# Opening of the linear attention: another order of norm, projections and evictions, with an early activation

## The chip, the core and the metric

The kernel runs on one core of a Trainium2 chip. The metric is the device time of one execution in microseconds (us). The engines of the core work beside each other and meet only at semaphores: PE (TensorE, matmuls and transposes; PEld is its weight load), DVE (VectorE), ACT (ScalarE), POOL (GpSimd) and SP (SyncE, which issues the DMAs). Each executes its own instructions strictly in the order of the program.

## The reference, cut to what matters

```python
def attn_a(hidden_states, ...):                        # hidden_states: layernorm(x), (2, 1024, 256)
    qkv = jax.nn.silu(hidden_states @ qkv_w.T)         # 32 heads of q, k and v, 64 each
    ...                                                # linear attention over blocks, with decays
    attn = _rmsnorm(attn, norm_w)
    gate = jax.nn.sigmoid(hidden_states @ gate_w.T)
    return gate * attn @ out_w.T

x = L0_attn_a_hidden_states                            # (2, 1024, 256) float32
x = x + attn_a(_layernorm(x), ...)                     # the stage of this change
x = x + ffn(_layernorm(x), ...)
x = x + attn_b(_layernorm(x), ...)
x = x + ffn(_layernorm(x), ...)
```

`_layernorm` subtracts the mean over the 256 features and divides by sqrt(variance + 1e-5).

## The kernel before

The 2048 tokens lie in SBUF as X, 16 tiles of 128 tokens by 256 features, in four blocks of four tiles (512 tokens). Every product of float32 matrices is made of three matmuls: each operand is split into a high part (rounded to the format that TensorE takes at full rate) and a low part (what the rounding left), and high by high, high by low and low by high are summed.

**The norm** (`norm_steps`) has a step for each block b and engine. `sync` loads the block. `moments` (DVE) takes statistics of four tiles (L84) and aggregates them (L87). `deviation` (ACT) takes the square root of the four variances (L93). `normalise` (DVE) takes the reciprocal (L97) and writes (x - mean) / deviation for four tiles (L100); in this stage the result lies in the buffer of the queries, so that the trace calls it la_q. `turn` (PE) transposes the four tiles in two halves of the features (L113), 8 transposes, into PSUM banks that are named la_Y and la_O in turn. `high` (ACT) copies both banks to a_hTh (L121), `low` (DVE) subtracts it from the bank and writes a_hTl (L127).

**The linear attention** (`linear_attention`) goes through 8 quads of heads, each in four steps of 512 tokens. A step needs projections (`project` on PE, L539) of kinds k, q, v and g (keys, queries, values, gate), in halves n = 0 and 1: k, q and g take 6 wide matmuls a half, v takes 12 of half the width. They alternate between two PSUM banks la_R. ACT evicts a bank (`evict`: L310 for k, L312 for q, L305 for v, L308 for g), through Silu or Tanh; the next use of that bank waits for it on the semaphore `silu_ok`. The weights of a quad come in four pieces (`PIECES`: queries and keys, values, gate, output). Each is split by `split` on ACT (L373, high part, semaphore `wh_ok`) and `low` on POOL (L245, low part, `wl_ok`). The projection of k waits for the first piece, that of v for the second.

ACT holds the functions of its activations in tables. The square root lies in another set than Silu and Tanh, so that an `ACT_TABLE_LOAD` stands in the program wherever it changes from the one to the other; plain copies need none.

**The order** is written out by hand for each engine: an opening in a straight line (the ends of the blocks `scalar`, `vector`, `tensor`, `gpsimd` before their loops), then a loop of units, one for each step. In the opening DVE norms block 0 and block 1 and then takes the low parts of block 0; PE turns both blocks, projects k and q of step 0 (four halves), turns block 2, computes scores, and projects v of step 0. ACT evicts these four halves after the deviation of block 3 and the split of the second piece. POOL takes the low part of the second piece only when all four blocks are normed (`h_ok`, NT = 16), and after it the decayed queries. SP issues in this order: block 0, the identity, the first piece of weights, block 1, the other pieces, the decays C, block 2, block 3.

Of the kernel before, what the change touches and what calls it, by code (L numbers as in the profile page):

```python
# [4 lines left out]
F32 = mybir.dt.float32  # L5
# [4 lines left out]
ACT = mybir.ActivationFunctionType  # L10
AXX = mybir.AxisListType.X

P = 128
BATCH, SEQ, HID = 2, 1024, 256
TOK = BATCH * SEQ
NT = TOK // P
KT = HID // P
TB = 512
NTB = TOK // TB
# [29 lines left out]
def norm_steps(nc, ctx, mem, name, X, ident, hTh, hTl, banks, load=None, norm=True, H=None):  # L49
# [4 lines left out]
    sb = lambda n, s, d: mem.enter_context(nc.sbuf_tensor(name + n, s, d))  # L54
    sem = lambda n: ctx.enter_context(nc.semaphore(name + n))
    if norm:
        stats = sb("stats", [P, NT, 6], F32)
        mv = sb("mv", [P, NT, 2], F32)
        std = sb("std", [P, NT], F32)
        rstd = sb("rstd", [P, NT], F32)  # L60
        epst = sb("epst", [P, 1], F32)
        eps_ok, stats_ok, mv_ok, std_ok = sem("eps_ok"), sem("stats_ok"), sem("mv_ok"), sem("std_ok")
        rstd_ok, h_ok = sem("rstd_ok"), sem("h_ok")
# [14 lines left out]
    def moments(dve, b):  # L78
# [6 lines left out]
        for t in range(TPB * b, TPB * (b + 1)):  # L85
            dve.wait_ge(stats_ok, t + 1)
            dve.bn_aggr(mv[:, t, :], stats[:, t, :]).then_inc(mv_ok, 1)  # L87

# [44 lines left out]
    return {"sync": sync, "moments": moments, "deviation": deviation, "normalise": normalise, "turn": turn,  # L133
# [3 lines left out]
def linear_attention(nc, ctx, X, ident, ident_in, hTh, hTl, hidden, w_quads, c_quads, ln2, fin, WF, w_ffn, q_ffn):  # L137

    with ExitStack() as mem:
        sb = lambda n, s, d: mem.enter_context(nc.sbuf_tensor("la_" + n, s, d))  # L140
# [100 lines left out]
        def _(pool):  # L241
# [36 lines left out]

            low(0, 0, 1)
# [20 lines left out]
        def _(act):  # L300
# [74 lines left out]
            for b in range(2):  # L375
                ln["deviation"](act, b)
            act.wait_ge(w0_in[0], 16)
            split(0)
            ln["high"](act, 0)
            ln["deviation"](act, 2)  # L380
            ln["high"](act, 1)
            ln["deviation"](act, 3)
            act.wait_ge(w0_in[1], 16)
            split(1)
            for n in range(4):
                evict(0, 0, "kq"[n // 2], n % 2, n)
# [30 lines left out]
        def _(dve):  # L417
# [91 lines left out]
            ln["moments"](dve, 0)  # L509
            ln["moments"](dve, 1)  # L510
            ln["normalise"](dve, 0)
            ln["normalise"](dve, 1)
            ln["low"](dve, 0)
            ln["moments"](dve, 2)
            ln["low"](dve, 1)
            ln["moments"](dve, 3)
            ln["normalise"](dve, 2)
            ln["normalise"](dve, 3)
            ln["low"](dve, 2)
# [15 lines left out]
        def _(pe):  # L535
# [168 lines left out]
            ln["turn"](pe, 0)  # L704
            ln["turn"](pe, 1)
            ln["ready"](pe, 0)
            for n in range(4):
                if n >= 2:
                    pe.wait_ge(silu_ok, n - 1)
                project(0, 0, "kq"[n // 2], n % 2)  # L710
# [1093 lines left out]
```

## Time and profile before

| | us |
|---|---|
| median of 3 runs | 1226.91 (1225.04 to 1227.93) |
| the profiled execution, its own time | 1230.14 |
| its span | 1228.1 |
| PE busy | 1123.5 (91%) |
| DVE busy | 652.6 (53%) |
| ACT busy | 594.7 (48%) |
| POOL busy | 486.8 (40%) |

The span is what the profiler saw from the first to the last instruction of that one execution. Busy times overlap, and a busy PE is not a PE at its peak, since matmuls are pipelined. PE carries most of the kernel; the exceptions are places where it waits for another engine, and the opening is one: in the first of forty equal slices of the span, PE is busy for four tenths, in the others mostly for nine or more.

### The profile page before, as it was taken

To read this page: it belongs to the slowest core of one execution; us is meant where nothing else is said; L and a number is where in the kernel's file an instruction comes from. 1 tells how busy PE (TensorE), PEld (TensorE's weight loads), DVE (VectorE), ACT (ScalarE), POOL (GpSimd) and SP (SyncE) were. 2 spreads that over 40 slices of the span, in tenths; PEclk is the share of its full clock that TensorE was granted. 3 is DMA by queue.
4 is the path that set the end of the run, shared out by engine and by line. 5 is a ranking of instruction groups with operands and counts; after the bars stand their busy time and mean duration, and the time that the engine had idled before them with its cause. 6 is when DMAs were issued, how large, how long until landed. Compare 5 with 4: busy or idle time off the path is not lost. (4 is left out here: it accounts for less than half of the span.)

```text
span 1228.1 us, 33277 instructions
## 1 busy us (share of the span) xinstructions
PE 1123.5 (91%) x14272; PEld 869.4 (71%) x14272; DVE 652.6 (53%) x1397; ACT 594.7 (48%) x1112; POOL 486.8 (40%) x513
## 2 busy tenths in 40 slices
PE   4999999999999999999987895894799999998698
PEld 3888888888888888888876785771344444436587
DVE  5243342433425455454467537885777777743742
ACT  3544444444445455554453442331367666774442
POOL 1445453454535546455453363104122222221255
PEclk8999999999999999999997897895899999999899
DMA  3100001001010020210301002155122222000001
GB/s 120 52 2 22 32 3 45 9 20 39 3 45 28 16 77 16 71 35 15 118 11 39 1 1 86 52 154 130 29 53 53 53 54 53 2 2 1 1 18 52
DMA packets 15805, 49.57 MB, mean 40 GB/s; under 512 B 2416, under 2 KB 7088, under 8 KB 12976
## 3 DMA queue, kind: packets, MB, share of 16 engines
q1 hardware_dynamic: 15664, 47.50, 13.3%
q8 instruction: 112, 1.84, 0.6%
q14 instruction: 29, 0.24, 0.1%
HBM read 36.54 MB, written 10.75 MB: 39 GB/s over the span
## 5 line engine op out<-in xcount | busy, mean ns | idle before, releaser
L1591 DVE TENSOR_REDUCE ca_mx<-ca_S 128x1 f32<-128x640 f32 (+1 forms) x192 | 177.4, 955 | 53.9 <-PE ca_S L1461 51.1
L1556 ACT ACTIVATE ca_PT<-ca_ST 128x512 f32<-128x512 f32 (+1 forms) x304 | 159.1, 578 | 81.2 <-PE ca_ST L1485 78.2
L451 DVE SCALAR_TENSOR_TENSOR la_y<-la_g,la_O 128x512 f32<-128x512 f32 x64 | 41.1, 684 | 221.6 <-PE la_O L627 221.6
L539 PE MATMUL la_R<-a_hTh,WF 128*128 128x512 f32 x384 | 131.0, 406 | 3.0 <-ACT la_k L310 3.0
L1432 POOL TENSOR_SCALAR_AFFINE_SELECT ca_PT<-ca_PT 128x256 f32<-128x256 f32 (+1 forms) x112 | 48.8, 442 | 193.0 <-ACT ca_PT L1556 192.7
L265 POOL TENSOR_TENSOR la_yl<-la_y,la_yh 128x512 fp32r<-128x512 f32 x64 | 81.8, 1299 | 94.5 <-ACT la_yh L339 94.5
L253 POOL TENSOR_TENSOR la_qd<-la_q,la_C 128x512 f32<-128x512 f32 x64 | 80.9, 1284 | 85.3 <-PE la_O L627 80.5
L458 DVE TENSOR_TENSOR X<-la_R,X 128x512 f32<-128x512 f32 x64 | 44.2, 691 | 119.8 <-PE la_R L539 119.7
L936 POOL TENSOR_TENSOR f_fl<-f_f,f_fh 128x512 fp32r<-128x512 f32 x48 | 62.5, 1308 | 112.2 <-ACT f_fh L840 112.2
L305 ACT ACTIVATE la_v<-la_R 128x512 f32<-128x512 f32 x64 | 38.3, 598 | 112.8 <-PE la_R L539 112.8
L442 DVE SCALAR_TENSOR_TENSOR la_S<-la_S,la_C,la_Y 128x64 f32<-128x64 f32 x448 | 88.7, 275 | 0.2
L539 PEld LDWEIGHTS la_R<-a_hTh,WF 128*128 128x128 f32 x384 | 74.1, 193 | 20.4 <-ACT la_k L310 3.5
L271 POOL TENSOR_TENSOR fin_sqacc<-fin_sqacc,la_sq 128x512 f32<-128x512 f32 x64 | 86.3, 1348 | 4.6
L312 ACT ACTIVATE la_q<-la_R 128x512 f32<-128x512 f32 x64 | 38.3, 599 | 102.7 <-PE la_R L539 102.7
L1499 PE MATMUL ca_OB<-ca_PT,V 128*32 128x512 f32 (+3 forms) x768 | 82.7, 502 | 3.2 <-POOL ca_PT L1432 1.6
L539 PE MATMUL la_R<-a_hTh,la_Wh 128*128 128x512 f32 x192 | 77.7, 405 | 0.0
L539 PE MATMUL la_R<-a_hTl,WF 128*128 128x512 f32 x192 | 76.8, 400 | 0.0
L539 PE MATMUL la_R<-a_hTh,la_Wl 128*128 128x512 f32 x192 | 76.2, 397 | 0.0
L539 PE MATMUL la_R<-a_hTl,la_Wh 128*128 128x512 f32 x192 | 75.9, 395 | 0.0
L1485 PE MATMUL ca_ST<-ca_QS,ca_KS 99*128 99x512 bf16 (+3 forms) x240 | 61.7, 328 | 3.2 <-ACT ca_PT L1556 1.4
L901 DVE SCALAR_TENSOR_TENSOR f_f<-f_U,SCL,f_sg 128x512 f32<-128x512 f32 x48 | 35.6, 748 | 51.8 <-PE f_U L789 40.2
L1458 PE MATMUL ca_S<-ca_KS,ca_QS 96*128 96x512 bf16 (+2 forms) x240 | 61.3, 329 | 2.0 <-DVE ca_mx L1591 1.9
(214 smaller groups left out, 2909.5 us busy)
## 6 DMA issues: line engine op xcount, KB each, us to landing
la_Wraw<-w_quads_dram SPq DMA_DIRECT2D x7, 1280.0 KB, 6.6
q_parts<-rp_QP SPq DMA_DIRECT2D x4, 768.0 KB, 3.7
k_parts<-rp_KP SPq DMA_DIRECT2D x4, 768.0 KB, 3.5
ca_KS<-k_parts SPq DMA_DIRECT2D x10, 256.0 KB, 6.8
qw_w<-w_ffn_dram SPq DMA_DIRECT2D x12, 192.0 KB, 2.4
q_ffn<-qw_w SPq DMA_DIRECT2D x12, 192.0 KB, 1.9
X<-hidden_dram SPq DMA_DIRECT2D x4, 512.0 KB, 7.3
out_dram<-X SPq DMA_DIRECT2D x8, 256.0 KB, 2.0
```

The costliest lines, as they stand in the source:

```text
L253: pool.tensor_tensor(qd[:, pr, :].rearrange("p (c t) -> p c t", t=CH), q[:, j % 4, pr, :].rearrange("p (c t) -> p c t", t=CH), C[:, slot, ...
L265: pool.tensor_tensor(yl[:, pr, :], y[:, pr, :], yh[:, pr, :].bitcast(F32), ALU.subtract).then_inc(yl_ok, 1)
L271: pool.tensor_tensor(sqacc[:, tok], sqacc[:, tok], sq[:, pr, :], ALU.add).then_inc(sqa_ok, 1)
L442: ins = dve.scalar_tensor_tensor(S[:, at, pr, :], S[:, at - 1, pr, :], C[:, slot, C_B + pr:C_B + pr + 1], U, ALU.mult, ALU.add)
L539: m = pe.matmul(out, a, b, start=n == 0, stop=n == len(pairs) - 1)
L936: pool.tensor_tensor(fl[:, tb % 2, it, :], f[:, n % 2, :], fh[:, tb % 2, it, :].bitcast(F32), ALU.subtract).then_inc(fl_ok, 1)
L1432: pool.affine_select(part, part, [[0, max(nh, 2)], [1, P]], ALU.is_ge, 0.0, base=0, channel_multiplier=-1).then_inc(cut_ok, 1)
L1458: ins = pe.matmul(bank[:, col:col + k1 - k0], Q[0:SROWS, j, qt * P:(qt + 1) * P], K[0:SROWS, j, k0:k1], start=True, stop=True)
L1485: ins = pe.matmul(ST[at % NB][:, e * w:(e + 1) * w], KS[g % NSL][0:KROWS, h + e, kt * P:(kt + 1) * P], QS[g % NSL][0:KROWS, h + e, q0:q0 + ...
L1499: ins = pe.matmul(OB[32 * j:32 * j + 32, q0 - qb * TB:q0 - qb * TB + w], V[:, 8 * (g % 2) + kt, HG * (g // 2) + j, :], PT[:, (NM2 * g + b) ...
L1556: act.activation(PT[:, (NM2 * g + b) % NPT, h:h + nh, 0:w], ST[at % NB][:, 0:nh * w].rearrange("p (h q) -> p h q", h=nh), ACT.Exp, scale=S ...
L1591: dve.reduce_max(out, src, AXX).then_inc(s1_free, 1)
```

## The change

Only the opening of the linear attention is touched; the loops and the other stages are the same.

- A new tile `root` (one number per partition) and a new step `table` of the norm: one activation with the square root of `epst`, which nobody reads. ACT begins with it.
- ACT: split of the first piece, then the deviation of block 1, the high parts of block 0, the deviations of blocks 2 and 3; then the evictions of k, the high parts of block 1, the evictions of q, and only then the split of the second piece.
- DVE: block 0 is normed before the moments of block 1; the moments of block 2 come before the low parts of block 0; then the moments of block 3 and the norms of blocks 1, 2 and 3; the low parts of block 1 follow them.
- PE: turns block 0 and projects k, then turns block 1 and projects q.
- POOL: its first split waits until block 0 is normed (`h_ok`, NT // NTB = 4).

```diff
@@ norm_steps
+    def table(act):
+        act.wait_ge(eps_ok, 1)
+        act.activation(root[:], epst[:], ACT.Sqrt, bias=epst[:])
@@ gpsimd
+            pool.wait_ge(ln["h_ok"], NT // NTB)
             low(0, 0, 1)
             pool.wait_ge(ln["h_ok"], NT)
             low(0, 1, 2)
@@ scalar
-            for b in range(2):
-                ln["deviation"](act, b)
+            ln["table"](act)
+            ln["deviation"](act, 0)
             act.wait_ge(w0_in[0], 16)
             split(0)
+            ln["deviation"](act, 1)
             ln["high"](act, 0)
             ln["deviation"](act, 2)
+            ln["deviation"](act, 3)
+            for n in range(2):
+                evict(0, 0, "k", n, n)
             ln["high"](act, 1)
-            ln["deviation"](act, 3)
+            for n in range(2):
+                evict(0, 0, "q", n, 2 + n)
             act.wait_ge(w0_in[1], 16)
             split(1)
-            for n in range(4):
-                evict(0, 0, "kq"[n // 2], n % 2, n)
             ln["high"](act, 2)
@@ vector
             ln["moments"](dve, 0)
+            ln["normalise"](dve, 0)
             ln["moments"](dve, 1)
-            ln["normalise"](dve, 0)
+            ln["moments"](dve, 2)
+            ln["low"](dve, 0)
+            ln["moments"](dve, 3)
             ln["normalise"](dve, 1)
-            ln["low"](dve, 0)
-            ln["moments"](dve, 2)
-            ln["low"](dve, 1)
-            ln["moments"](dve, 3)
             ln["normalise"](dve, 2)
             ln["normalise"](dve, 3)
+            ln["low"](dve, 1)
             ln["low"](dve, 2)
@@ tensor
             ln["turn"](pe, 0)
+            ln["ready"](pe, 0)
+            for n in range(2):
+                project(0, 0, "k", n)
             ln["turn"](pe, 1)
-            ln["ready"](pe, 0)
-            for n in range(4):
-                if n >= 2:
-                    pe.wait_ge(silu_ok, n - 1)
-                project(0, 0, "kq"[n // 2], n % 2)
+            for n in range(2):
+                pe.wait_ge(silu_ok, n + 1)
+                project(0, 0, "q", n)
             ln["turn"](pe, 2)
```

In the compiled program the order on ACT, from its first instruction on, was as follows. std is the deviation, WF the high part of the weights, x_in, mv_ok, std_ok and t_ok are semaphores of load, moments, deviation and turn.

```order
L93 ACT_TABLE_LOAD [waits ln1_mv_ok]
L93 ACTIVATE ln_std<-ln_mv,ln_epst 128x4 [waits ln1_eps_ok]
L93 ACTIVATE ln_std<-ln_mv,ln_epst 128x4 [waits ln1_mv_ok]
L373 ACTIVATE WF<-la_Wraw 128x1024 [waits la_w0_in0]
L121 ACTIVATE a_hTh<-la_Y 128x512 [waits ln1_t_ok] x2
L93 ACTIVATE ln_std<-ln_mv,ln_epst 128x4 [waits ln1_mv_ok]
L121 ACTIVATE a_hTh<-la_O 128x512 [waits ln1_t_ok] x2
L93 ACTIVATE ln_std<-ln_mv,ln_epst 128x4 [waits ln1_mv_ok]
L373 ACTIVATE WF<-la_Wraw 128x512 [waits la_w0_in1]
L310 ACT_TABLE_LOAD
L310 ACTIVATE la_k<-la_R 128x512 [waits la_proj_ok] x2
L312 ACTIVATE la_q<-la_R 128x512 [waits la_proj_ok] x2
```

In the changed kernel the same part of ACT reads:

```order
L91 ACT_TABLE_LOAD
L91 ACTIVATE ln_root<-ln_epst 128x1 [waits ln1_eps_ok]
L97 ACTIVATE ln_std<-ln_mv,ln_epst 128x4 [waits ln1_mv_ok,ln1_eps_ok]
L379 ACTIVATE WF<-la_Wraw 128x1024 [waits la_w0_in0]
L97 ACTIVATE ln_std<-ln_mv,ln_epst 128x4 [waits ln1_mv_ok]
L125 ACTIVATE a_hTh<-la_Y 128x512 [waits ln1_t_ok] x2
L97 ACTIVATE ln_std<-ln_mv,ln_epst 128x4 [waits ln1_mv_ok] x2
L316 ACT_TABLE_LOAD
L316 ACTIVATE la_k<-la_R 128x512 [waits la_proj_ok] x2
L125 ACTIVATE a_hTh<-la_O 128x512 [waits ln1_t_ok] x2
L318 ACTIVATE la_q<-la_R 128x512 [waits la_proj_ok] x2
L379 ACTIVATE WF<-la_Wraw 128x512 [waits la_w0_in1]
```

The first table load waits for nothing now; the deviation of block 3 has moved up to that of block 2, the split of the second piece (the last row) from in front of the evictions to behind them.

On DVE the part behind the moments of block 0 was as follows; la_q is the normed block, a_hTl the low part.

```order
L84 BN_STATS ln_stats<-X 128x6 [waits ln1_x_in1]
L84 BN_STATS ln_stats<-X 128x6 x3
L87 BN_AGGR ln_mv<-ln_stats 128x2 [waits ln1_stats_ok] x4
L97 RECIPROCAL ln_rstd<-ln_std 128x4 [waits ln1_std_ok]
L100 TENSOR_SCALAR la_q<-X,ln_mv,ln_rstd 128x256 [waits ln1_rstd_ok]
L100 TENSOR_SCALAR la_q<-X,ln_mv,ln_rstd 128x256 x3
L97 RECIPROCAL ln_rstd<-ln_std 128x4 [waits ln1_std_ok]
L100 TENSOR_SCALAR la_q<-X,ln_mv,ln_rstd 128x256 [waits ln1_rstd_ok]
L100 TENSOR_SCALAR la_q<-X,ln_mv,ln_rstd 128x256 x3
L127 TENSOR_TENSOR a_hTl<-la_Y,a_hTh 128x512 [waits ln1_hi_ok] x2
L84 BN_STATS ln_stats<-X 128x6 [waits ln1_x_in2]
```

In the changed kernel it reads:

```order
L101 RECIPROCAL ln_rstd<-ln_std 128x4 [waits ln1_std_ok]
L104 TENSOR_SCALAR la_q<-X,ln_mv,ln_rstd 128x256 [waits ln1_rstd_ok]
L104 TENSOR_SCALAR la_q<-X,ln_mv,ln_rstd 128x256 x3
L84 BN_STATS ln_stats<-X 128x6 [waits ln1_x_in1]
L84 BN_STATS ln_stats<-X 128x6 x3
L87 BN_AGGR ln_mv<-ln_stats 128x2 [waits ln1_stats_ok] x4
L84 BN_STATS ln_stats<-X 128x6 [waits ln1_x_in2]
L84 BN_STATS ln_stats<-X 128x6 x3
L87 BN_AGGR ln_mv<-ln_stats 128x2 [waits ln1_stats_ok] x4
L131 TENSOR_TENSOR a_hTl<-la_Y,a_hTh 128x512 [waits ln1_hi_ok] x2
L84 BN_STATS ln_stats<-X 128x6 [waits ln1_x_in3]
```

The norm of block 0 stands in front of the moments of block 1. The statistics of block 2, which wait for its transfer (x_in2), now stand in front of the low parts of block 0.

## Rows read from the trace of the kernel before

**Rows 1.** Timeline, 5 to 17 us: start us, duration us, engine, line, operation, idle before.

```profile
5.17 1.40 DVE L84 BATCH_NORM_STATS2 ln_stats<-X 128x6 f32<-128x256 f32 x4 [4.24 <-DMA X<-hidden_dram]
...
6.94 1.28 ACT L93 ACT_TABLE_LOAD   x1 [6.94 <-DVE ln_mv L87]
8.23 0.30 ACT L93 ACTIVATE ln_std<-ln_mv,ln_epst 128x4 f32<-128x4 f32 x1
8.62 1.40 DVE L84 BATCH_NORM_STATS2 ln_stats<-X 128x6 f32<-128x256 f32 x4 [1.77 <-DMA X<-hidden_dram]
...
10.41 1.38 DVE L100 TENSOR_SCALAR la_q<-X,ln_mv,ln_rstd 128x256 f32<-128x256 f32 x4
...
11.66 2.35 POOL L245 TENSOR_TENSOR WF<-la_Wraw,WF 128x1024 fp32r<-128x1024 f32 x1 [11.16 <-ACT WF L373]
...
11.91 3.22 DVE L100 TENSOR_SCALAR la_q<-X,ln_mv,ln_rstd 128x256 f32<-128x256 f32 x4
...
15.05 1.28 DVE L127 TENSOR_TENSOR a_hTl<-la_Y,a_hTh 128x512 fp32r<-128x512 f32 x2
...
15.19 1.97 PE L113 MATMUL la_O<-ident,la_q 128*128 128x128 f32 x8 [1.31 <-DVE la_q L100]
...
16.81 0.78 PE L539 MATMUL la_R<-a_hTh,WF 128*128 128x512 f32 x1
```

**Rows 2.** Instructions of tile X on SP, 4 to 5 us, and their time to landing.

```profile
L74 SPq DMA_DIRECT2D X<-hidden_dram x1: 1021/1021/1021, 4.1 to 4.1; - x1
...
DMA to landing us min/median/max: 8.5/8.5/8.5
```

**Rows 3.** Timeline, 19 to 33 us.

```profile
19.95 0.54 PE L539 MATMUL la_R<-a_hTl,WF 128*128 128x512 f32 x1
...
21.89 0.61 ACT L373 ACTIVATE WF<-la_Wraw 128x512 fp32r<-128x512 f32 x1
22.52 1.28 ACT L310 ACT_TABLE_LOAD   x1
...
24.47 0.79 PE L539 MATMUL la_R<-a_hTh,WF 128*128 128x512 f32 x1 [3.05 <-ACT la_k L310]
...
24.72 1.28 POOL L245 TENSOR_TENSOR WF<-la_Wraw,WF 128x512 fp32r<-128x512 f32 x1 [10.70 <-DVE la_q L100]
...
27.43 0.60 ACT L312 ACTIVATE la_q<-la_R 128x512 f32<-128x512 f32 x1 [2.53 <-PE la_R L539]
...
31.09 1.16 PE L593 MATMUL la_SC<-la_q,la_k 64*64 64x64 f32 x64
...
32.18 0.50 PE L539 MATMUL la_R<-WF,a_hTh 128*128 128x256 f32 x2
```

**Rows 4.** Stretches on PE: from:to, length, busy (instructions), granted clock, DMA share, GB/s.

```profile
24.47:29.70 5.23, 5.23 (x12) 0.50 0.00 0
...
30.30:31.00 0.70, 0.70 (x7) 0.85 0.00 0
...
32.18:56.20 24.02, 24.02 (x266) 1.00 0.17 65
41.40:44.40 3.00, 3.00 (x137) 1.00 0.02 5
```

**Rows 5.** Timeline, 35 to 43 us.

```profile
35.82 0.48 PE L539 MATMUL la_R<-a_hTh,WF 128*128 128x512 f32 x1
...
37.49 0.60 ACT L310 ACTIVATE la_k<-la_R 128x512 f32<-128x512 f32 x1 [0.93 <-PE la_R L539]
...
38.86 0.60 ACT L310 ACTIVATE la_k<-la_R 128x512 f32<-128x512 f32 x1
...
41.42 1.04 PE L113 MATMUL la_O<-ident,la_q 128*128 128x128 f32 x8
```

**Rows 6.** Timeline of DVE and of POOL in a later stage, at 671 us.

```profile
670.51 1.39 DVE L84 BATCH_NORM_STATS2 ln_stats<-X 128x6 f32<-128x256 f32 x4
...
671.34 1.29 POOL L936 TENSOR_TENSOR f_fl<-f_f,f_fh 128x512 fp32r<-128x512 f32 x1 [1.81 <-ACT f_fh L840]
```

More of the change, by code:

```diff
@@ L60, in norm_steps @@
         rstd = sb("rstd", [P, NT], F32)
-        epst = sb("epst", [P, 1], F32)
+        epst, root = sb("epst", [P, 1], F32), sb("root", [P, 1], F32)
         eps_ok, stats_ok, mv_ok, std_ok = sem("eps_ok"), sem("stats_ok"), sem("mv_ok"), sem("std_ok")
@@ L131, in ready @@
         pe.wait_ge(lo_ok, KT * (b + 1))
-    return {"sync": sync, "moments": moments, "deviation": deviation, "normalise": normalise, "turn": turn,
+    return {"sync": sync, "moments": moments, "table": table if norm else None,
+            "deviation": deviation if norm else None, "normalise": normalise, "turn": turn,
             "high": high, "low": low, "ready": ready, "h_ok": h_ok if norm else None}
```

## The prediction

> **What bounds the kernel now.** I read the timeline of the opening first, then the busy time and granted clock by stretch, then the timeline of the stretch behind. The reader is to look for the first moment from which TensorE has no holes. That moment is 32.18 us, the first matmul of the values of step 0 [rows 3]: from there to the first unit of the main loop at 56.2 us TensorE is busy 24.02 of 24.02 us at granted clock 1.00 [rows 4]. Nothing in the kernel is tied to the start of the span later than the input transfers, all waits are relative, and so what the opening gains or loses in front of that matmul is what the kernel gains or loses. The diff touches only the opening; the order of everything behind it is the same.
>
> How is 32.18 made up? The first block of X is there at 5.17, its moments release ScalarE at 6.94, ScalarE loads a table for 1.28 us, and the deviation follows at 8.23. VectorE has gone on to the moments of block 1 at 8.62 and so norms block 0 only at 10.41 and block 1 at 11.91. The latter takes 3.22 us instead of 1.38, since GpSimd's weight split runs from 11.66 to 14.01 [rows 1]. The low parts of block 0 come at 15.05 to 16.33, and TensorE, which turns block 1 first (15.19), projects the first keys at 16.81 [rows 1]. The twelve matmuls of the keys are done at 21.4, and then TensorE is idle until 24.47: the evictions of the keys stand on ScalarE behind the deviation of block 3, a split and the second table load at 22.52 [rows 3]. In this hole the granted clock falls: it is 0.50, the lower of its two levels (1.2 of 2.4 GHz), from 24.47 to 29.70, where the twelve matmuls of the queries take 5.23 us, and rises at about 30.5 (0.85 over 30.30 to 31.00) [rows 4]. Then turn, scores, and 32.18.
>
> **The change, part by part.** I follow the new order from landing to the first matmul of the values. Each step is max(what it waits for), plus its own duration.
>
> The early table. The load (1.28) and one tiny activation (the smallest activation shown, 0.30) move into ScalarE's idle time before 6.94 [rows 1]; the program has the load ahead of the wait, so it is hidden, and the deviation of block 0 runs at 6.94 to 7.24. The norm of block 0 follows at about 7.5 (the reciprocal needs 0.2 to 0.3) and ends at 8.9, against 11.8. If the load were not hidden, 1.3 us would come back here, but the next paragraph shows that this has cover.
>
> The wait on block 2. Behind the norm VectorE takes the moments of block 1 (landed by 8.62; a block takes 1.7, from 5.17 to 6.94 [rows 1]): 8.9 to 10.6. Then come the moments of block 2, now ahead of the low parts of block 0. That transfer was issued at 4.1 and needed 8.5 us [rows 2]: it lands at 12.65. In the kernel before nobody waited for it. So the moments of block 2 end at 14.35, and only then come the two subtractions of the low parts (1.28), to 15.65, though TensorE's turn (9.0 to 11) and the high parts (until about 11.6) have long been ready. Queued behind this wait on VectorE are the low parts, and behind them TensorE. The first keys start at 15.7 instead of 16.81: of the 2.9 us gained on the norm only 1.1 is left. The 2 us on the norm and the 1.3 of the table are cover, not gain.
>
> The wait on GpSimd. Its first split now waits for the norm of block 0 and runs at 9.0 to 11.35 (2.35 [rows 1]). It is needed at 15.7: free. With it the norm of block 0 is clear of GpSimd, and the other norms fall where GpSimd waits anyway, so the extra 1.84 us of row 11.91 goes.
>
> The keys. Twelve matmuls from 15.7, at the lower level of the clock: 0.43 each, 12 in 5.23 [rows 4]. When does the level rise? Before, it was 3.3 us after the first wide matmul (16.81 to about 20.1: the matmul at 19.95 lasts 0.54, between the 0.63 of the slow and the 0.40 of the fast ones; the clock column shows 1.00 there all along, so I go by durations) [rows 1, 3] and 6.0 us after the second start (24.47 to 30.5) [rows 4]. I take the middle, 4.65: at 20.35, and the keys are through at 20.6. Ends: at 19.0, through at 20.0; at 21.7, through at 20.8 with a slow turn behind.
>
> ScalarE meanwhile. The moments of block 3 come after the low parts (15.65 to 17.35), its deviation to 17.7, the table load to 19.0 (1.28), the first keys' eviction (ready at 15.7 + 2.96 = 18.7, as 24.47 to 27.43 [rows 3]) at 19.0 to 19.6. This bank is wanted at 21.6, so 2 us of cover. This is where the 3 us hole was: TensorE now turns block 1 (1.04, row 41.42 [rows 5]) at 20.6 to 21.65, its norm being done at about 19.1.
>
> The queries at the full clock. Six matmuls take 1.38 (distance of the evictions 37.49 and 38.86 [rows 5]), twelve 2.76: 21.65 to 24.4, against 5.23. Turn of block 2 and scores: 1.04 and 1.1 (31.09 to 32.18 [rows 3]), so TensorE is free at 26.55.
>
> A new wait. The second split of the weights now stands on ScalarE behind the queries' evictions, and GpSimd's part of it behind that. From the end of the queries' matmuls: 0.3 to the eviction (1.67 from first matmul to eviction at 37.49, less 1.38 [rows 5]), 0.6 for it, 0.61 for the split (row 21.89), 1.28 on GpSimd (row 24.72 [rows 3]), and 0.15 of hand-overs: 2.95. So the values start at 24.4 + 2.95 = 27.35; TensorE waits 0.8 for GpSimd. Before, this split had been done at 26.0, six us early.
>
> The sum: 32.18 - 27.35 = 4.85 us. With the ends of the rise 26.75 and about 27.9, that is 5.4 and 4.3. Behind it the relations are those of before: the high parts of block 2 and the third split come at about the same distance from the values, and GpSimd's decayed queries earlier. Nothing is late next except TensorE itself. One tile of 4 bytes per partition is added; I price it at nothing.
>
> The sum is against the profiled execution: its span of 1228.1, and its time of 1230.14, minus 4.85 gives 1225.3. But the median of the runs is 1226.91, 3.2 less, so the ordinary run has some luck that this one had not. One place for it is the slow stretch that I remove: had the clock risen 3.3 and not 6.0 us after 24.47, as the first time, 2.7 us at half speed would have cost 1.35 less, and the gain would be 3.5. Between 3.5 and 4.85 I take 4.2: 1226.91 - 4.2 = **1222.7 us**.
>
> **Rivals.**
>
> 1. **The clock falls in front of the values.** Between the queries' last wide matmul and the values lie a turn, the scores and 0.8 us of waiting, 2.95 us in all; a hole of 3 us made it fall before. Against: over 41.40 to 44.40 TensorE did only a turn, state sums and scores, and the granted clock stayed 1.00 [rows 4]. Price: up to 6.0 us at half speed, 3.0. Time 1222.7 + 3.0 = 1225.7. The Trainium skill says in "TensorE: Matmul & The Clock Gate", Part 4: PE-mode transpose, that a transpose does not count as TensorE being busy in the way a matmul does. By that rule the two turns would be holes, and this rival likelier. The trace's stretch at 1.00 speaks mildly against it, since only 1.04 of its 3.0 us were transposes.
>
> 2. **VectorE is shut out by GpSimd.** GpSimd's split at 9.0 to 11.35 lies on the moments of block 1. If they were held as the norm at 11.91 was [rows 1], they would end at 13.1, those of block 2 at 14.8, the low parts at 16.1: 0.45 later, 1223.2. Against: statistics at 670.51 took 1.39 for four, as always, with GpSimd subtracting from 671.34 on [rows 6]. The Trainium skill, "SBUF — State Buffer", section SBUF: two separate sides, says the shared ports are an exclusive lock for GpSimd against VectorE instructions in a two-port mode or with two SBUF inputs. The norm's 3.22 agrees with it; the statistics of rows 6 do not show themselves as such an instruction.
>
> 3. **The gain is given back later**: the loop is paced by something that I took to be relative, and the early start is waited off, 1226.9. Against it is the gapless stretch of rows 4.
>
> 4. **Slower: block 2 comes late.** The one new wait on a transfer: every microsecond that block 2 lands after 12.65 delays low parts, keys and all behind by one, because VectorE is already waiting there from 10.6. The kernel before has 3.6 us of cover at this place (its moments of block 2 start at 16.33 or so, behind the low parts). The gain is gone if it lands 4.2 later, at 16.9; from 6.7 later, at 19.3, the kernel is slower by over 0.2%: about 1229.5. For: it is issued behind six others. Against: no transfer is added or moved, 8.5 us was already under full load, and nothing in the change asks for half as much again.
>
> 5. **It does not do what it says**: the table load would still come late. Covered, as shown: nothing.
>
> **How the numbers follow.** A measurement of this kernel can tell about 0.2%, 2.5 us, from no change. Forecast 0.68, clock 0.12, shut out 0.08, given back 0.06, late transfer 0.06. Faster by over 2.5 us: most of the forecast (0.62 of 0.68, as its lower end of 3.5 is only 1.0 above the bound), 0.06 of the second, 0.02 of the first: 0.70. Slower: half of the fourth, and 0.02 for given back with noise: 0.05, with 0.25 left in between. Range: below, 5.4 us and 1.3 for the spread of the runs, 1220.2; above, the clock's fall and the same spread, cut at 1226.6.
>
> **What would show it.** In the profile after: a table load before 3 us; norm of block 0 ending at 8.9; statistics of block 2 starting at 12.7 after a wait for the transfer; the first wide matmul at 15.7; no idle time over 1 us on TensorE between keys and queries; queries in 2.8 us at clock 1.00; the first matmul of the values at 27.35, released by GpSimd. I am wrong if the clock row shows 0.50 after 22, if block 2 lands elsewhere than at 12.65, or if the distance from the values to the first loop unit is not 24.0 to 24.3.

## The result, and the profile after

| | kernel before | changed kernel |
|---|---|---|
| first comparison, median | 1227.42 us (4 runs) | 1220.38 us (4 runs) |
| ratio, 95% interval | | 0.9944 (0.9926 to 0.9962) |
| second comparison, median | 1227.69 us (17 runs) | 1222.14 us (12 runs) |
| ratio, 95% interval | | 0.9952 (0.9934 to 0.9969) |
| span of the profiled execution | 1228.1 us | 1216.9 us |

The changed kernel is faster by 7.0 us in the first comparison (4.7 to 9.1 us by its interval) and by 5.6 us in the second, larger one (3.8 to 8.1 us), against a forecast of 4.2 us. The profiled spans differ by 11.2 us; in the profiles below the opening accounts for only 4.5 to 5.3 us of this.

First the opening of the changed kernel up to the first keys (timeline: start us, duration us, engine, line, operation, and in brackets the idle time before it and who ended it). Lines behind L87 have moved by 4 or more: L97 is the deviation, L104 the norm, L131 the low parts, L548 the projections, L250 the weights' low parts.

```profile
0.79 1.28 ACT L91 ACT_TABLE_LOAD   x1 [0.79 <-PEq L1804]
...
5.38 1.41 DVE L84 BATCH_NORM_STATS2 ln_stats<-X 128x6 f32<-128x256 f32 x4 [4.45 <-DMA X<-hidden_dram]
...
7.16 0.30 ACT L97 ACTIVATE ln_std<-ln_mv,ln_epst 128x4 f32<-128x4 f32 x1 [4.77 <-DVE ln_mv L87]
...
7.70 1.38 DVE L104 TENSOR_SCALAR la_q<-X,ln_mv,ln_rstd 128x256 f32<-128x256 f32 x4
...
9.23 2.35 POOL L250 TENSOR_TENSOR WF<-la_Wraw,WF 128x1024 fp32r<-128x1024 f32 x1 [8.73 <-DVE la_q L104]
9.28 1.41 DVE L84 BATCH_NORM_STATS2 ln_stats<-X 128x6 f32<-128x256 f32 x4 [0.20 <-DMA X<-hidden_dram]
...
13.14 1.41 DVE L84 BATCH_NORM_STATS2 ln_stats<-X 128x6 f32<-128x256 f32 x4 [2.18 <-DMA X<-hidden_dram]
...
14.74 1.26 DVE L131 TENSOR_TENSOR a_hTl<-la_Y,a_hTh 128x512 fp32r<-128x512 f32 x2
...
16.05 0.79 PE L548 MATMUL la_R<-a_hTh,WF 128*128 128x512 f32 x1 [4.88 <-DVE a_hTl L131]
```

The table load stands at 0.79 and the deviation follows the moments at 7.16 (before: 6.94 and 8.23 [rows 1]). The norm of block 0 ends at 9.08 instead of 11.79. GpSimd begins at 9.23, beside the statistics of block 1, which take 1.41 as ever. Then VectorE waits 2.18 us for block 2, and only behind its moments come the low parts (14.74) and the keys (16.05, before 16.81).

Then from the keys to the values:

```profile
17.95 1.28 ACT L316 ACT_TABLE_LOAD   x1
...
19.24 0.60 ACT L316 ACTIVATE la_k<-la_R 128x512 f32<-128x512 f32 x1
19.63 0.71 PE L548 MATMUL la_R<-a_hTh,WF 128*128 128x512 f32 x2
...
20.66 1.03 PE L117 MATMUL la_O<-ident,la_q 128*128 128x128 f32 x8
...
21.45 0.48 PE L548 MATMUL la_R<-a_hTh,WF 128*128 128x512 f32 x1
...
24.99 0.62 ACT L379 ACTIVATE WF<-la_Wraw 128x512 fp32r<-128x512 f32 x1
...
25.26 1.16 PE L602 MATMUL la_SC<-la_q,la_k 64*64 64x64 f32 x64
...
25.75 1.27 POOL L250 TENSOR_TENSOR WF<-la_Wraw,WF 128x512 fp32r<-128x512 f32 x1 [14.16 <-ACT WF L379]
...
27.17 0.48 PE L548 MATMUL la_R<-WF,a_hTh 128*128 128x256 f32 x2 [0.75 <-POOL WF L250]
```

The clock rises at the matmuls of 19.63 (two of them take 0.71, between 1.05 and 0.62). The table load at 17.95 ends at 19.23, about 0.2 us after the first half of the keys is ready (an eviction comes 2.96 us behind the first matmul where ScalarE is free, 24.47 to 27.43 [rows 3], which makes 19.01 here), and the first eviction stands right behind it; this costs nothing, since the bank is wanted only at 21.45. The turn of block 1 fills the place where TensorE had stood idle for 3.05 us [rows 3]. The queries start at 21.45, and the values at 27.17, after a wait of 0.75 us for GpSimd, whose own work hangs on the split at 24.99. The stretches, as in [rows 4] (from:to, length, busy time and instructions of TensorE, granted clock, DMA share, GB/s):

```profile
21.40:24.20 2.80, 2.80 (x15) 1.00 0.00 0
24.20:27.17 2.97, 2.22 (x74) 1.00 0.02 6
27.17:51.50 24.33, 24.33 (x260) 1.00 0.18 64
```

The twelve matmuls of the queries lie in 2.8 us at granted clock 1.00, where they took 5.23 us at 0.50 [rows 4]. From the values to the first unit of the loop it is 24.35 us (27.17 to 51.52), and before it was 24.30 (32.18 to 56.48). So the opening is shorter by 5.01 us, and what is behind it starts 4.96 us earlier.

Where are the other 6.2 us of the profiled spans? The times at which the same instructions start in both traces differ by 4.96 at the first unit, by 5.7 at the last sums of the linear attention, and by 10.95 at the stores of the rotary projections. The change has no instruction in there. This is the stretch between the last sums and the first store of the keys' projections, in the kernel before:

```profile
657.10:800.95 143.85, 119.34 (x611) 0.88 0.11 38
```

and in the changed kernel:

```profile
651.40:790.00 138.60, 115.32 (x611) 0.90 0.11 40
```

143.85 against 138.60 us, with granted clock 0.88 against 0.90. The experiments ask how much of this is chance.

### The profile page after: what moved, and what is told of

The parts are those of the page before. It is cut to its first block and busy times, and to the rows that moved or that the text cites. A ratio compares the mean times of both kernels' runs of the same rounds, so it can differ in the third digit from the quotient of the medians.

```text
span 1216.9 us, 33279 instructions
## 1 busy us (share of the span) xinstructions
PE 1114.9 (92%) x14272; PEld 863.4 (71%) x14272; DVE 650.5 (53%) x1397; ACT 596.1 (49%) x1113; POOL 486.3 (40%) x513
## 3 DMA queue, kind: packets, MB, share of 16 engines
q8 instruction: 112, 1.84, 0.6%
## 5 line engine op out<-in xcount | busy, mean ns | idle before, releaser
L548 PE MATMUL la_R<-a_hTh,WF 128*128 128x512 f32 x384 | 129.2, 401 | 4.9 <-DVE a_hTl L131 4.9
L548 PEld LDWEIGHTS la_R<-a_hTh,WF 128*128 128x128 f32 x384 | 73.0, 190 | 22.6 <-DVE a_hTl L131 5.3
L548 PE MATMUL la_R<-a_hTh,la_Wh 128*128 128x512 f32 x192 | 77.3, 403 | 0.0
L548 PE MATMUL la_R<-a_hTl,WF 128*128 128x512 f32 x192 | 76.1, 396 | 0.0
L548 PE MATMUL la_R<-a_hTh,la_Wl 128*128 128x512 f32 x192 | 75.8, 395 | 0.0
L548 PE MATMUL la_R<-a_hTl,la_Wh 128*128 128x512 f32 x192 | 75.7, 394 | 0.0
L316 ACT ACTIVATE la_k<-la_R 128x512 f32<-128x512 f32 x64 | 38.4, 600 | 48.5 <-PE la_R L548 48.4
```

The source lines that it names most:

```text
L548: m = pe.matmul(out, a, b, start=n == 0, stop=n == len(pairs) - 1)
```

## The experiments

Behind the opening all kernels have the same program, that of the kernel before as of the changed one. So each profile gives two numbers: when the values start, which is the opening's and repeats to 0.3 us in the changed kernel and 0.5 us in the one before, and how long the later stages take, which says how large the noise is. Seven kernels were timed once: block2_early 1215.73 us, no_table 1218.83, no_table_no_wait 1218.86, split_early 1220.75, norm_first_alone 1224.46, before_root 1225.65 and warm 1225.70. The kernel before alone spreads from 1222.47 to 1230.74, so these single times decide little, and the start times in the profiles are what is read.

### Is the wait for block 2 what binds the opening?

**low_first** exchanges two lines of VectorE in the changed kernel:

```diff
             ln["moments"](dve, 1)
+            ln["low"](dve, 0)
             ln["moments"](dve, 2)
-            ln["low"](dve, 0)
             ln["moments"](dve, 3)
```

> The changed kernel with two lines of VectorE exchanged: the low parts of block 0 come before the moments of block 2. My theory: the opening of the changed kernel is bound by the wait for the transfer of block 2 (VectorE sat idle 2.18 us there, from 10.96 to 13.14), and the low parts behind it. Then the low parts start when the high parts are done, about 12.3, the first keys at about 13.7 instead of 16.05, and the first matmul of the values moves from 27.17 to 24.8 (24.3 to 25.6, by when the clock rises). Rival: the start of the keys was not the limit but the chain over ScalarE (deviation of block 3, table load, evictions), so that the keys start earlier but the values move by under 1 us.

VectorE and TensorE of low_first, timeline:

```profile
11.37 1.29 DVE L131 TENSOR_TENSOR a_hTl<-la_Y,a_hTh 128x512 fp32r<-128x512 f32 x2 [0.85 <-ACT a_hTh L125]
...
12.71 0.79 PE L548 MATMUL la_R<-a_hTh,WF 128*128 128x512 f32 x1 [1.70 <-DVE a_hTl L131]
...
23.93 0.47 PE L548 MATMUL la_R<-WF,a_hTh 128*128 128x256 f32 x2 [0.75 <-POOL WF L250]
```

The low parts come at 11.37, the keys at 12.71 and the values at 23.93: 3.2 us earlier than in the changed kernel, more than I expected, because the keys could start at 12.7 and not at 13.7 (the low parts need only the first of the two high parts to begin, and began at 11.4 and not at 12.3). The values come even before the range that I had given (24.3 to 25.6). The median of 6 runs is 1217.66 us against 1225.58 us of before (9 runs), ratio 0.9926 (0.9899 to 0.9952). The theory holds.

**block2_early** leaves VectorE alone and moves the transfer:

```diff
+            ln["sync"](sp, 2)
             sp.dma_start(Wraw[:, W_V:WTOT], w_quads[0, :, W_V:WTOT]).then_inc(w0_in[1], 16)
             sp.dma_start(C[:, 0, :], c_quads[0, :, :]).then_inc(c_in[0], 16)
-            for b in range(2, NTB):
-                ln["sync"](sp, b)
+            ln["sync"](sp, 3)
```

> The changed kernel with the transfer of block 2 issued ahead of the second piece of weights and of the decays. The same theory by another way: block 2 lands at about 10.5 to 11 instead of 13.1, VectorE doesn't wait, its moments are done at 12.7, low parts at 14.0, first keys at 14.0, values at 25.1. Rival (transfers are only exchanged, and what comes later is then late): the second piece of weights lands after 12 but is wanted at about 25, so it can't bind; if the values stay at 27, the wait was not what bound them.

Its statistics of block 2, first keys and values:

```profile
11.25 1.37 DVE L84 BATCH_NORM_STATS2 ln_stats<-X 128x6 f32<-128x256 f32 x4
...
14.13 0.80 PE L548 MATMUL la_R<-a_hTh,WF 128*128 128x512 f32 x1 [2.69 <-DVE a_hTl L131]
...
25.01 0.47 PE L548 MATMUL la_R<-WF,a_hTh 128*128 128x256 f32 x2 [0.75 <-POOL WF L250]
```

No wait stands in front of the statistics of block 2 (11.25), and the values come at 25.01 as expected (25.1). Two different edits that take the wait away both bring the opening forward; that is the cause shown. Five profiles with the wait left in give the same thing without any edit. The statistics of block 2 start when it lands, and the keys follow:

| kernel | statistics of block 2, us | first keys, us | difference |
|---|---|---|---|
| after_again | 12.57 | 15.48 | 2.91 |
| no_table | 13.00 | 15.91 | 2.91 |
| warm | 13.02 | 15.93 | 2.91 |
| changed kernel | 13.14 | 16.05 | 2.91 |
| split_early | 13.45 | 16.36 | 2.91 |

### What do the early table and GpSimd's wait bring?

**no_table** takes `ln["table"](act)` out of the changed kernel.

> The changed kernel without the early activation, so that the first table load stands behind the moments of block 0. My theory: 1.3 us later up to the norm of block 0, which ends at 10.4, then covered by the wait for block 2: first keys at 16.05 as in the changed kernel, values at 27.2, no loss. Rival: the loss goes through, values at 28.5.

Norm of block 0 and statistics of block 2:

```profile
8.90 1.38 DVE L104 TENSOR_SCALAR la_q<-X,ln_mv,ln_rstd 128x256 f32<-128x256 f32 x4
...
13.00 1.41 DVE L84 BATCH_NORM_STATS2 ln_stats<-X 128x6 f32<-128x256 f32 x4 [1.12 <-DMA X<-hidden_dram]
```

The norm is 1.2 us later than at 7.70, and VectorE still waits 1.12 us for block 2. The values come at 27.34 against 27.17. The keys start at 15.91, 2.91 us behind those statistics, so the 0.17 us between the values is not the table's. The early table gains nothing by itself here: it fills a wait. In low_first, where that wait is gone, it was not tried without the table.

**no_table_no_wait** also takes out GpSimd's wait for the norm of block 0:

```diff
-            ln["table"](act)
-            pool.wait_ge(ln["h_ok"], NT // NTB)
```

> As the one before, and GpSimd's first split no longer waits for the norm of block 0. My theory: the split begins at about 9.2, the norm of block 0 (9.0 to 10.4) is held for about 2.2 us in one of its instructions, and so the norm ends at about 12.6, the moments of block 1 at 14.3, those of block 2 at 16.0, the low parts at 17.3, keys at 17.4: the values move to about 28.5, 1.3 later. Rival: GpSimd comes second and is held itself, the norm ends at 10.4, and nothing moves.

VectorE and GpSimd:

```profile
8.64 3.40 DVE L104 TENSOR_SCALAR la_q<-X,ln_mv,ln_rstd 128x256 f32<-128x256 f32 x4
...
15.13 1.25 DVE L131 TENSOR_TENSOR a_hTl<-la_Y,a_hTh 128x512 fp32r<-128x512 f32 x2
...
9.42 2.48 POOL L250 TENSOR_TENSOR WF<-la_Wraw,WF 128x1024 fp32r<-128x1024 f32 x1 [8.91 <-ACT WF L378]
```

The norm takes 3.40 us instead of 1.38 while GpSimd subtracts from 9.42 to 11.90; as in row 11.91 of [rows 1], it is held. So these two engines meet not only at semaphores. But the low parts come only 0.39 us later than in the changed kernel (15.13 against 14.74) and the values 0.70 (27.87), since the 1.1 us of waiting for block 2 absorbs part of it. I had expected 28.5: the norm started at 8.64 and not at 9.0, was held for 2.0 us and not 2.2, and the moments of the two blocks took 1.6 us each and not 1.7. The wait for block 2 thus hides most of what both edits together protect against. GpSimd's wait was not taken out alone. With the early table in, it depends on the landing of the weights whether it has anything to protect: in the changed kernel's profile ScalarE's split ends at 9.09 and the norm at 9.08, so that GpSimd could not have begun before the norm was done; in after_again, where the weights were there sooner, the split ends at 8.18 and the norm at 8.85, and without the wait it would have.

### The wait in front of the values

**split_early** moves the split of the second piece in the changed kernel:

```diff
             ln["deviation"](act, 3)
+            act.wait_ge(w0_in[1], 16)
+            split(1)
             for n in range(2):
                 evict(0, 0, "k", n, n)
@@
-            act.wait_ge(w0_in[1], 16)
-            split(1)
             ln["high"](act, 2)
```

> The changed kernel with ScalarE's split of the second piece of weights right behind the deviation of block 3 instead of behind the evictions of the queries. My theory: the wait that the change put in front of the values (TensorE idle 0.75 us, released by GpSimd at 27.17) goes, and nothing takes its place, since the keys' evictions become only 0.6 later and their banks are wanted at 21.4; values at 26.4 instead of 27.17. Rival: the evictions of the keys become late and with them the queries, so that the values stay at 27.

```profile
22.46 1.29 POOL L250 TENSOR_TENSOR WF<-la_Wraw,WF 128x512 fp32r<-128x512 f32 x1 [10.40 <-DVE la_q L104]
...
26.24 0.50 PE L548 MATMUL la_R<-WF,a_hTh 128*128 128x256 f32 x2
```

GpSimd now waits only for the last norm (22.46), and the values start at 26.24 without idle time in front of them, although block 2 had landed 0.3 us later than in the changed kernel. Its clock rose earlier behind the first keys, so that the keys were through at 20.55 (20.66 in the changed kernel); counted from there, the values come 0.82 us sooner. The wait of 0.75 us was real and went; the theory holds.

### The start alone

**norm_first_alone** puts the first part of the change into the kernel before:

```diff
-            for b in range(2):
-                ln["deviation"](act, b)
+            ln["table"](act)
+            ln["deviation"](act, 0)
             act.wait_ge(w0_in[0], 16)
             split(0)
+            ln["deviation"](act, 1)
@@ vector
             ln["moments"](dve, 0)
+            ln["normalise"](dve, 0)
             ln["moments"](dve, 1)
-            ln["normalise"](dve, 0)
@@ gpsimd
+            pool.wait_ge(ln["h_ok"], NT // NTB)
             low(0, 0, 1)
```

> The first part of the change alone, put into the kernel before: early activation, block 0 normed before the moments of block 1, GpSimd's wait. TensorE still turns block 1 before the keys, and the evictions of the keys stand behind the deviation of block 3, the split and the table load. My theory: the keys start at about 14.7, two us earlier than before, but the hole before the queries stays (2 us or more), the clock falls or not by its luck, and the values come at 27.5 (clock stays) to 30 (it falls): so between a half and all of the gain of 5.0 comes from the start, the rest from the hole. Rival: the start is hidden by the evictions altogether, values at 31 or later.

TensorE: turn of block 1, first keys, first queries, values.

```profile
12.94 1.97 PE L117 MATMUL la_O<-ident,la_q 128*128 128x128 f32 x8 [2.00 <-DVE la_q L104]
14.56 0.78 PE L546 MATMUL la_R<-a_hTh,WF 128*128 128x512 f32 x1
...
22.22 0.79 PE L546 MATMUL la_R<-a_hTh,WF 128*128 128x512 f32 x1 [3.01 <-ACT la_k L316]
...
29.97 0.50 PE L546 MATMUL la_R<-WF,a_hTh 128*128 128x256 f32 x2
```

The keys start at 14.56, 1.5 us before those of the changed kernel, since here the low parts of block 0 do not wait for block 2. But the hole in front of the queries is still 3.01 us, the queries run at the lower clock (12 in 5.2 us at granted clock 0.50), and the values come at 29.97. So an early start gives 2.2 of the 5.0 us, less than the half that I had named as the least. Block 1 came later here than in the profile of before: its statistics start at 9.25 after 0.39 us of waiting, against 8.62. Without that wait the start would be worth about 2.6 us (an estimate, 2.2 and 0.39). The changed kernel gets the rest, 2.4 to 2.8 us, by closing the hole, in spite of a later start of the keys.

### The clock

**warm** adds transposes that nobody reads to the changed kernel:

```diff
+            def warm(n):
+                for _ in range(n):
+                    pe.transpose(R[0][:, 0:P], ident[:], ident[:])
+
+            pe.wait_ge(ln["id_in"], 16)
+            warm(16)
             ln["turn"](pe, 0)
+            warm(22)
             ln["ready"](pe, 0)
```

> The changed kernel with 38 additional transposes of the identity, whose results nobody reads: 16 before the turn of block 0 (from about 5.5 us on) and 22 between this turn and the keys. It asks two things. First, what the lower clock at the keys costs: if the transposes raise the clock, the twelve matmuls of the keys are 0.23 apart, take 2.8 us from 16.05 instead of 4.6, and the values move from 27.17 to about 26.0 (the evictions of the keys, at 19.2, hold back part of it). Second, whether transposes count for the clock: if they do not, the first matmuls of the keys are 0.43 apart as before and the values stay at 27.2, or come later if the transposes run into the keys.

```profile
5.45 3.67 PE L716 MATMUL la_R<-ident 128*128 128x128 f32 x16 [5.45 <-DMA ident<-ident_dram]
...
10.24 2.56 PE L716 MATMUL la_R<-ident 128*128 128x128 f32 x22
15.93 0.51 PE L549 MATMUL la_R<-a_hTh,WF 128*128 128x512 f32 x1 [3.13 <-DVE a_hTl L131]
...
19.92 0.39 PE L549 MATMUL la_R<-a_hTl,WF 128*128 128x512 f32 x1
```

and the stretch in which the first keys run:

```profile
16.50:19.50 3.00, 3.00 (x8) 0.50 0.00 0
```

The second batch of transposes is at the full clock: 22 take 2.56 us, 0.12 each, where the first 16 take 3.67, 0.23 each. So transposes alone raised the clock; they count. But TensorE then waits 3.13 us for the low parts, the clock falls at about 16.4 (granted 0.50 from 16.5 to 19.5), and the keys gain next to nothing: they are through at 20.38, in the changed kernel at 20.66, and the values come at 26.90. The experiment answers its second question and leaves the first open, since the keys never ran at the full clock. Its single time (1225.70 us) is above all runs of the changed kernel; 1.0 us of it is idle or slower time of TensorE between values and loop (25.29 instead of 24.3), 0.6 us of which the profile puts down to instruction issue at 40.8. Why the added instructions do that I did not find out.

### The later stages: change or luck?

**before_root** is the kernel before with the additional 4-byte tile and nothing else.

> The kernel before with nothing but the additional tile of 4 bytes per partition, which shifts the tiles behind it. The profiled executions differed by 11.2 us in span, of which the opening has 5.0; 5.2 lie between the last sums of the linear attention and the stores of the rotary projections. My theory: that is the granted clock of these stretches, which differs from execution to execution; here the stretch takes anything between 138 and 144 us, the opening has its values at 31 to 32.2. Rival: the shift of the tiles makes the later stages faster, and the stretch is at 139 to 140 here too while the times are 2 us or more below the runs of before.

The stretch from the last sums to the stores:

```profile
656.40:796.67 140.27, 116.59 (x611) 0.89 0.11 39
```

It takes 140.27 us here, without the changed opening and 3.6 us less than in the first profile of before; the time, 1225.65 us, lies inside the 1222.47 to 1230.74 us of the unchanged kernel. By itself this fits both the theory of chance and the rival of the tile.

**after_again** is the changed kernel once more, unchanged.

> The changed kernel again, unchanged, on the same chip and in the same rounds as the one above. It was 7.0 us faster by medians where the opening explains 5.0, and its profile 11.2. My theory: the rest is the spread of the later stages; a second profile has the values at 27.0 to 27.5 again, but the stretch from the last sums to the stores of the rotary projections at anything from 138 to 144 us, and the gain by medians is nearer to 5 us (ratio 0.995 to 0.997). Rival: the gain is 7 us, ratio 0.994, since something in the change also makes the later stages faster.

```profile
26.88 0.47 PE L548 MATMUL la_R<-WF,a_hTh 128*128 128x256 f32 x2 [0.75 <-POOL WF L250]
...
650.50:792.62 142.12, 115.02 (x611) 0.90 0.11 39
```

The same program, with the same tile, now takes 142.12 us for the stretch that took 138.60. So it is not the tile. Over the twelve profiles of this study the stretch lies between 138.60 and 143.85 us; the first two profiles, of the changed kernel and of the one before, happened to be its two ends. The time goes with the granted clock: the five fastest of the twelve runs of after_again have a mean clock of 0.963 to 0.967, the five slowest 0.957 to 0.960. That does not account for all of it: low_first has 141.36 us at 0.92, more than the 138.60 at 0.90. What else varies there stays open. The values of after_again come at 26.88, and its gain by medians is 5.6 us: the theory's 5 and not the 7 of the first comparison, though the interval (3.8 to 8.1 us) does not exclude 7.

### Both waits away

**low_and_split** is low_first with the split between the high parts of block 1 and the evictions of the queries:

```diff
             ln["high"](act, 1)
+            act.wait_ge(w0_in[1], 16)
+            split(1)
             for n in range(2):
                 evict(0, 0, "q", n, 2 + n)
-            act.wait_ge(w0_in[1], 16)
-            split(1)
```

> The changed kernel with both waits that it put in front of TensorE taken away: low parts of block 0 ahead of the moments of block 2, and the split of the second piece of weights between the high parts of block 1 and the evictions of the queries. My theory: the keys start at 12.7 to 13.7, TensorE has no idle time from there on, and the values come at 23.2 to 23.6 instead of 27.17: 3.5 to 4 us less than the changed kernel and 8.5 to 9 less than the one before, ratio to before about 0.993. Rival: the later stages give part of it back, and the ratio is that of the changed kernel alone, 0.995 or more.

GpSimd, and TensorE from the keys to the values:

```profile
20.57 1.30 POOL L250 TENSOR_TENSOR WF<-la_Wraw,WF 128x512 fp32r<-128x512 f32 x1 [9.15 <-ACT WF L379]
...
12.76 0.80 PE L548 MATMUL la_R<-a_hTh,WF 128*128 128x512 f32 x1 [1.70 <-DVE a_hTl L131]
...
17.62 0.63 PE L548 MATMUL la_R<-a_hTh,WF 128*128 128x512 f32 x1
18.05 1.17 PE L117 MATMUL la_O<-ident,la_q 128*128 128x128 f32 x8
...
23.89 0.50 PE L548 MATMUL la_R<-WF,a_hTh 128*128 128x256 f32 x2
```

GpSimd is done at 21.87, two microseconds before it is needed, and from 12.76 on TensorE has no idle time. But the values start at 23.89, no earlier than in low_first (23.93) and behind the 23.2 to 23.6 that I had expected. The clock rose later: all twelve matmuls of the keys and part of the turn are slow here (0.63 at 17.62), while in low_first it rose at 16.3 to 16.8. This costs the 0.7 us that the second edit brings. Compared side by side, low_and_split takes 1217.45 us (6 runs), after_again 1222.14 us (12 runs) and the kernel before 1227.69 us (17 runs): ratio to before 0.9933 (0.9911 to 0.9954). By medians it is 4.7 us better than the changed kernel; the opening explains 3.0 to 3.3 of that, and the rest is within the spread of the later stages. Whether the second edit adds to the first cannot be told from these runs.

## Why the prediction was right

The path and its places were right; here is each step. Two of the signs by which the prediction called itself wrong were met, both by a little: block 2 landed at about 13.1 and not at 12.65, and the distance from the values to the loop was 24.35 us, where 24.0 to 24.3 was said.

- **The early table**: loaded at 0.79, hidden, and worth nothing behind the wait for block 2. Shown by no_table, where VectorE still waits 1.12 us.
- **The wait for block 2**: predicted as the one new wait, with the keys at 15.7. It landed at 13.1 instead of 12.65, and the keys came at 16.05. The rival "block 2 comes late" is thereby seen at work, 1 to 1 as said, but over 0.9 us in five profiles and not over the 4.2 that would have eaten the gain. The sum left 1.1 of the 2.9 us that the norm had gained, 0.8 were left, and low_first shows what the wait costs in all: without it the keys start 3.3 us earlier.
- **GpSimd's wait**: free. The loss that it guards against is real (3.40 instead of 1.38 us in no_table_no_wait), but in the changed kernel's profile, with the early table in, there was nothing to guard, as said there; the "1.84 us" that the prediction counts as gone is that of block 1, whose norm now stands where GpSimd is idle (1.39 us at 17.69).
- **Rise of the clock**: 3.3 to 6.0 us after the first wide matmul, taken as 4.65; it was about 3.8 (16.05 to 19.9). The keys started 0.35 us late and the clock rose 0.45 us early; that these two errors cancelled, and the keys were through at 20.65 (forecast 20.6), was luck.
- **Keys' evictions and the hole**: at 19.24 (forecast 19.0), turn at 20.66 (20.6), queries 21.45 (21.65).
- **The new wait in front of the values**: 0.75 us (0.8), values at 27.17 (27.35). In the profile the opening gained 5.0 us where the sum had 4.85.
- **The rivals**: the clock did not fall in front of the values, and warm shows that transposes raise it. The statement of the Trainium skill, "TensorE: Matmul & The Clock Gate", Part 4: PE-mode transpose, that they do not count as TensorE being busy, disagrees with warm: 0.12 instead of 0.23 us per transpose after 16 of them and a turn. VectorE's statistics were not shut out by GpSimd (1.41 beside it at 9.28); the norm was (3.40 in no_table_no_wait). This agrees with the exclusive lock between VectorE and GpSimd of which the Trainium skill tells in "SBUF — State Buffer", section SBUF: two separate sides, if the norm is an instruction of the kind that takes the shared ports; no run here shows that. The price of this rival, 0.45 us, was too high by its own comparison: with the 1.84 us that the norm had lost, the moments of block 1 would have ended at about 12.45, before block 2 landed, and nothing would have moved.

What stays open is the last term, by which the forecast (4.2 us) differs from the sum (4.85 us). I took 0.65 us off for luck that the profiled run of before had not had in the slow stretch that the change removes. A second profile of the same opening, before_root, shows such luck: the statistics of block 1, the first keys, the first queries and the values.

```profile
9.32 1.40 DVE L84 BATCH_NORM_STATS2 ln_stats<-X 128x6 f32<-128x256 f32 x4 [2.64 <-DMA X<-hidden_dram]
...
17.52 0.78 PE L539 MATMUL la_R<-a_hTh,WF 128*128 128x512 f32 x1
...
25.17 0.50 PE L539 MATMUL la_R<-a_hTh,WF 128*128 128x512 f32 x1 [3.71 <-ACT la_k L310]
...
31.68 0.50 PE L539 MATMUL la_R<-WF,a_hTh 128*128 128x256 f32 x2
```

Here the clock fell at about 26.3, within the queries, and not ahead of them. From the first query to the values it takes 6.51 us, where the profiled run of before took 7.71 (24.47 to 32.18): 1.20 us of luck, close to the 1.35 us at which the prediction priced it. The values are only 0.5 us earlier because block 1 had landed 0.70 us later (9.32 against 8.62 [rows 1]). This shows a wait that the prediction did not name: the kernel before waited for block 1 as the changed kernel waits for block 2. VectorE was idle for it (1.77 and 2.64 us), and in both profiles the first keys come 8.2 us and the first queries 15.85 us behind those statistics.

So the two profiles of before differ in two draws that nearly cancel. Against the two of the changed kernel (27.17 and 26.88) the opening gains 4.5 to 5.3 us; had both been good or both bad, it would be about 3.8 to 6.0 us (an estimate: the values of before at 31.0 or 32.9). How often the clock behaves in the one way or the other, two profiles do not say. The 5.6 us of the second comparison (3.8 to 8.1) fits the 4.2 of the forecast and the 4.85 of the sum alike; the 7.0 of the first has 4.7 as its lower end and leaves the 4.2 just outside. The mechanism is shown; that the forecast was that near to the measured median is partly luck. The later stretch of the profile of before, 143.85 us, is 3.2 us above the median of the twelve profiles (140.6), and that is about as much as its time was above the median of the runs.

## What to carry to other kernels

When a step is moved forward, look at what it now passes that did not have to wait before: here two lines that set statistics in front of the low parts made the whole opening wait for a transfer that nobody had been waiting for, and exchanging them gave another 3.2 us. Ask the same of the order as it stands: the kernel before hung on the landing of block 1, and norming block 0 first took that wait out of the way of the keys. Close holes in TensorE's work; a hole of 3 us cost its own length and then up to 2.5 us more, because the matmuls behind it ran at the lower clock (the queries took 5.23 us instead of 2.8; 4.3 in before_root). And where profiled spans differ by more than the changed part explains, compare the start times of the same instructions stage by stage and take a second profile before explaining the rest.

## What the runs showed of the hardware

- Transposes alone raised TensorE's clock: from 0.23 to 0.12 us each (warm).
- A hole of 3.0 to 3.7 us lowered it in all four profiles whose opening had one between wide matmuls or behind transposes at the full clock (before, norm_first_alone, before_root, warm), with the lower level beginning anywhere from inside the hole (21.5, norm_first_alone) to 1.1 us behind its end (26.3, before_root).
- The rise came 2.0 to 6.0 us after the first wide matmul of a stretch, at different distances for the same program (3.8 in the changed kernel and 4.4 in after_again, 3.3 in the kernel before and 2.0 in before_root, which differs by one tile) and for openings that differ in other places (2.8 in split_early, 5.5 in low_and_split, 6.0 behind the hole of the kernel before). In low_and_split this alone cost 0.7 us against low_first.
- The same transfers landed at different times: the statistics that waited for block 1 began between 8.62 and 9.77 us, those that waited for block 2 between 12.57 and 13.45 us, in kernels that issue them in the same order.
- While GpSimd subtracted, VectorE's norm of four tiles took 3.22 to 3.40 us instead of 1.38, and the statistics of four tiles 1.39 to 1.41, as always.
